# The exponential of an attention step split by head, and its scores issued after its value product

## What is computed

```python
L_q = exterior(q1, q2); L_k = exterior(k1, k2)      # 6 numbers per head and position, of length 1
scores = einsum('bqhc,bkhc->bhqk', L_q, L_k @ _J6.T) * 6.0 ** -0.5
attn = softmax(where(causal, scores, -inf))
out = einsum('bhqk,bkhd->bqhd', attn, v) @ W_out.T  # d = 64
x = x + out + ffn(xn)
```

## Time and profile before

| | |
|---|---|
| time before, median of 2 runs (4733.71 to 4743.04) | 4738.38 us |
| the profiled execution: its time, and the span of its slowest core | 4758.37 us, 4757.3 us |
| spans of the eight cores | 4691.6 to 4757.3 us |
| busy, share of the span: PE, PEld, DVE, ACT, POOL | 60%, 21%, 29%, 31%, 3% |
| exponentials (L580) | 1280, 1120.0 us busy, ScalarE idle before them 2099.5 us |
| value matmuls (L597) | 2560, 1037.8 us busy, TensorE idle before them 842.6 us |
| score matmuls (L557) | 2560, 618.3 us busy, TensorE idle before them 429.4 us |
| masks (L588) | 512, 143.2 us busy |
| divides, first activation (L621) | 128, 130.2 us busy |

### The profile page before, as it was taken

One profiled execution on the slowest core, in us unless ns is written; L12 is line 12 of the kernel. 1 busy time (PEld: TensorE's weight loads), 2 busy tenths in 40 slices (PEclk: granted clock), 3 DMA queues, 4 the chain that ended last, 5 costly groups with the idle time before them and its releaser, 6 DMA issues.

```text
span 4757.3 us, 36021 instructions; the slowest of 8 cores (4691.6 to 4757.3 us)
## 1 busy us (share of the span) xinstructions
PE 2870.3 (60%) x10528; PEld 995.3 (21%) x10528; DVE 1385.6 (29%) x2833; ACT 1475.0 (31%) x1729; POOL 139.4 (3%) x210
## 2 busy tenths in 40 slices
PE   2258555566656855556655865656665586666665
PEld 1115111122112511112211421111221151111112
DVE  4524434322222333332322333332222231111111
ACT  0000144443331034443433014443342203455450
POOL 1200000000000000000000010000000000000001
PEclk9957655567655865566766875556775695555558
DMA  5501310111100320111100041001110021000004
GB/s 110 47 0 54 96 33 27 34 58 62 49 9 7 47 44 27 34 38 62 67 27 11 5 73 34 27 27 56 62 58 7 5 45 36 14 12 14 12 12 73
DMA packets 87144, 180.26 MB, mean 38 GB/s; under 512 B 41760, under 2 KB 42920, under 8 KB 86960
## 3 DMA queue, kind: packets, MB, share of 16 engines
q0 software_dynamic: 56672, 75.38, 8.3%
q1 hardware_dynamic: 30288, 102.58, 7.4%
HBM read 114.36 MB, written 69.73 MB: 39 GB/s over the span
## 4 chain that ended last, share of the span: by engine, by line
PE 44%; DMA 21%; DVE 14%; ACT 12%; issue 7%; DVEq 0%; SPq 0%; ACTq 0%; POOLq 0%; POOL 0%
PE O L597 17%; DMA cdiv<-rscr 10%; DMA y<-ost 7%; PE S L557 7%; PE F L401 5%; ACT exps L580 5%; PE F L437 4%; DMA rscr<-cdiv 3%; DVE oT L639 3%; ACT cdiv L623 3%; ACT cdiv L621 3%; PE F L444 3%; PE F L327 2%; DVE exps L588 1%; DVE stat L278 1%
## 5 line engine op out<-in xcount | busy, mean ns | idle before, releaser
L580 ACT ACTIVATE exps<-S 128x1024 bf16<-128x1024 f32 (+3 forms) x1280 | 1120.0, 894 | 2099.5 <-PE O L597 1354.4
L597 PE MATMUL O<-exps,vaug 128*65 128x512 bf16 (+3 forms) x2560 | 1037.8, 506 | 842.6 <-DVE oT L639 500.1
L557 PE MATMUL S<-fqp,fkp 6*128 6x512 bf16 (+3 forms) x2560 | 618.3, 492 | 429.4 <-ACT exps L580 422.7
L597 PEld LDWEIGHTS O<-exps,vaug 128*65 128x65 bf16 x2560 | 230.3, 136 | 1284.2 <-issue 1265.7
L639 DVE TENSOR_TENSOR oT<-O,cdiv 64x512 bf16<-64x512 f32 x256 | 175.0, 684 | 922.4 <-DMA cdiv<-rscr 916.6
L557 PEld LDWEIGHTS S<-fqp,fkp 6*128 6x128 bf16 x2560 | 141.0, 97 | 1145.4 <-issue 1139.7
L588 DVE TENSOR_TENSOR exps<-exps,tri 128x256 bf16<-128x256 bf16 x512 | 143.2, 290 | 734.9 <-ACT exps L580 732.0
L506 PE MATMUL S<-wout,oT 128*128 128x512 bf16 x1024 | 260.6, 416 | 87.0 <-DVE ost L515 77.6
L401 PE MATMUL F<-wv,xnT 128*128 128x256 bf16 x2048 | 259.0, 291 | 0.6 <-DVE vaug L413 0.3
L307 PE MATMUL F<-idt,xnst 128*128 128x128 f32 x512 | 121.7, 417 | 156.8 <-DVE xnst L294 156.8
L401 PEld LDWEIGHTS F<-wv,xnT 128*128 128x128 bf16 x2048 | 202.0, 103 | 62.6 <-issue 20.9
(11 more groups left out here) (72 smaller groups left out, 1962.6 us busy)
## 6 DMA issues: line engine op xcount, KB each, us to landing
y<-ost POOLq DMA_DIRECT2D x128, 512.0 KB, 5.2
xst<-x SPq DMA_DIRECT2D x64, 512.0 KB, 4.3
x2st<-x SPq DMA_DIRECT2D x64, 512.0 KB, 4.1
cdiv<-rscr SPq DMA_DIRECT2D x128, 256.0 KB, 3.7
wv<-wvT POOLq DMA_DIRECT2D x8, 256.0 KB, 19.8
wout<-woutT POOLq DMA_DIRECT2D x8, 256.0 KB, 20.2
tascr<-qk POOLq DMA_DIRECT2D x16, 128.0 KB, 2.0
rscr<-cdiv SPq DMA_DIRECT2D x128, 4.0 KB
```

The costliest lines, as they stand in the source:

```text
L557: tS.inc(TE.matmul(S_ps[:, ss * 1024 + j * 512 + soff: ss * 1024 + j * 512 + 512], fk_pad[32 * m4:32 * m4 + 6, kt * 128:kt * 128 + 128], f ...
L580: sS.inc(SE.activation(e_out, e_in, AF.Exp))
L597: ins = TE.matmul(O4[:, j * 512 + off:(j + 1) * 512], vaug[:, kt * 1040 + h * 65: kt * 1040 + h * 65 + 65], exp_sb[:, ss * 1024 + j * 512 ...
```

## The change

The body of the step loop in `C_pair` is written anew. The exponential, the mask and the value product are done for one head after the other: two exponentials of up to 512 columns in place of one of up to 1024, two masks of 128 columns in place of one of 256, and a wait of each value matmul for its own head's exponential or mask. Each value matmul counts on its semaphore, where only the second did. S(kt + 2) is issued behind the value product of kt, where it was ahead of it. The buffers, `emit_scores`, the divide and `pace()` are as before. `pace()` is still called at the end of the step.

```diff
             for kt in range(nkt):
                 off = max(kt * 128 - w * 512, 0)
                 ss = kt % 2
-                tS.wait(SE, max(av_snap[kt - 2], sc_snap[kt]))
-                ... (e_out, e_in: both heads, an access pattern of [2, 512 - off])
-                sS.inc(SE.activation(e_out, e_in, AF.Exp))
+                for j in range(2):
+                    base = ss * 1024 + j * 512 + off
+                    end = ss * 1024 + (j + 1) * 512
+                    tS.wait(SE, max(avj.get((kt - 2, j), av_snap.get(kt - 2, 0)), sc_snap[kt]))
+                    sS.inc(SE.activation(exp_sb[:, base:end], S_ps[:, base:end], AF.Exp))
+                    ej = sS.n
+                    if kt >= 4 * w:
+                        sS.wait(VE, ej)
+                        in0 = exp_sb[:, base: base + 128]
+                        mk = vS.inc(VE.tensor_tensor(in0, in0, tri_sb[:, 0:128], OP.mult))
+                        vS.wait(TE, mk)
+                    else:
+                        sS.wait(TE, ej)
+                    if kt == 0 and j == 0:
+                        vS.wait(TE, stx["o4_free"])
+                    m4 = 2 * pr + j
+                    h = 4 * g + m4
+                    tS.inc(TE.matmul(
+                        O4[:, j * 512 + off:(j + 1) * 512],
+                        vaug[:, kt * 1040 + h * 65: kt * 1040 + h * 65 + 65],
+                        exp_sb[:, base:end],
+                        start=(kt == 0), stop=(kt == last_kt)))
+                    avj[(kt, j)] = tS.n
                 exp_snap[kt] = sS.n
+                av_snap[kt] = tS.n
                 if kt + 2 < nkt:
                     emit_scores(kt + 2)
-                if kt >= 4 * w:
-                    ... (one mask of both heads; TensorE waits for it)
-                elif kt + 2 >= nkt:
-                    sS.wait(TE, exp_snap[kt])
-                if kt == 0:
-                    vS.wait(TE, stx["o4_free"])
-                for j in range(2):
-                    ... (the same two value matmuls; tS.inc behind the second)
```

More of the change, by code:

```diff
@@ L569, in C_pair @@
                 stx["pending_div"] = None
+            avj = {}
             for kt in range(nkt):
@@ L602, in C_pair @@
-                tS.inc(ins)
-                av_snap[kt] = tS.n
                 if pace is not None:
```

## The result

| | before | changed |
|---|---|---|
| time, median (runs) | 4742.63 us (10) | 4807.01 us (11) |
| ratio to before, 95% interval | | 1.0147 [1.0124, 1.0170] |
| profiled execution, span of the slowest core | 4757.3 us | 4828.1 us |
| spans of the eight cores, mean | 4723 us | 4804 us |

The change costs 64 us by the medians (70 by the ratio), where 39 were forecast. It stays within 2%, and its interval lies wholly above 1.

The account below looks back on a forecast made before the run. TensorE was taken as the bound at the slow clock, the score-exponential round trip at the fast one. Tail loss of 49 us less 10 gained in fast steps gave +39: 4777 us against the 4738 median, range 4715 to 4835.

Parts of the forecast that it names:

- Full steps, halves, waits: Unmasked steps at the slow clock: stay 1.53 us; half exponentials 0.60 us; extra waits taken as 0, at most 38 us.
- The rule weighed there: ScalarE's exponentials: each split adds some 93 ns, by that alone 119 us over 1280 splits, a sum near 4857.
- The tail: Last masked steps of a pair: late scores add 0.44 us to longer pairs, 0.20 to 4-step pairs, 49 us in all.
- Fast steps: Full steps at the fast clock: halves close the round trip sooner, 1.03 us for 1.10, 144 steps, 10 us gained.
- Moving S(k+2) behind AV(k): Score matmuls issued after value matmuls: middle of a pair unchanged, bill only at its end, +0.44 or +0.20 us per pair.
- The split's worth: Exponential by head: no gain in full slow-clock steps, 10 us gained at the fast clock.
- Round trips vanish: Rival, score matmuls' wait for the exponential: 338 of 422.7 us cost nothing; losing the other 85 gives 4653; chance 0.08.
- A gap between the two heads: Rival, between a step's two value matmuls: the new wait costs 0.14 us, 1280 times, 179 us, giving 4956; chance 0.06.
- ACT becomes the bound: Rival, ScalarE's half exponentials: 4816 if halves don't overlap, 4879 if ScalarE were the bound everywhere; chance 0.04.
- The clock rises: Rival, slow full steps in the last batch and elsewhere: denser TensorE work keeps 2.4 GHz, 192 us gained, 4585; chance 0.02.

Follow-up runs that it names:

- e4: Changed kernel with pace() called between the value product of kt and the scores of kt + 2, so a block follows value matmuls; 1.0030 of the kernel before.
- e2: Kernel before with only the scores of kt + 2 moved behind the value product of kt, exponential and mask left whole; 1.0243 of the kernel before.
- a couple: Split by head in the old order, with two key tiles' scores issued together, then their four value matmuls; four exponential slots, bf16 bias; 0.9443 of the kernel before.

## Why the prediction was right and wrong

**Full steps, halves, waits.** Right. Full steps at 0.50 stay 1.53 us, halves take 0.59, AV of both heads 1.06 as before, so the wait between the heads costs nothing that shows, and the last batch's clock stays 0.50. The rule weighed there, of the Trainium skill, ScalarE: Activation LUTs, section "What ACT_TABLE_LOAD costs", would have put 93 ns on each split, an estimate from its figures. ScalarE's busy time grew by 61 ns each, and none of it lies on the path, as the prediction read from its trace.

**The tail.** Right: 5.69 us for 5.68, 3.70 for "some 3.7", the last batch's stage 709.6 for 708. In the other batches it costs less than taken (28.8 us in e4 for 36), and why is open.

**Fast steps.** Right in size (2.05 us for two, 2.06 forecast). In e4 the full steps of batches 0 to 2 gain 9.6 us, forecast 10, and that is luck in part: a fast step gained 0.04 us where 0.07 was taken, and 6 more steps were fast. In the changed kernel they gain 3.2, because 19 fewer of them per core are fast.

**What failed** is the step *Moving S(k+2) behind AV(k)*. It followed S and AV of the pair, and asked of the clock only whether denser work might raise it. It didn't ask what is queued behind the moved instruction: `pace()` stands at the end of the step, so a block of full-row work that had followed AV now follows S, and its clock rises later. This term was put at nothing. It is +35.6 us in the steps with a block, +44 us in the profiles against e4 (3474.5 - 3430.3) and 55 by the ratios. Less than half of what the steps lost against e4 lies inside the blocks (16.8 of 37.9 us), the rest is S itself, now run at the slow clock. Without the term, e4 stands where the forecast's own terms lead: the tail 14.4 + 28.8, less 9.6 for fast steps, less 7 between pairs and in steps with blocks, +26 in the profiles (14 by the ratio, which goes by the slowest core) where 39 was forecast. The missing term makes it 71 in the profiles. That the measured time still lies inside the stated range is luck: its upper part was made of 38 us for the waits and 20 for the half exponentials and masks, and neither came.

**The split's worth** was under-sized too. As a part by itself it gives 2.2%, where the prediction had 10 us for it at the fast clock and nothing elsewhere: in the old order it shortens the diagonal as well (518.2 us against 557.9), and in the stages with blocks more steps are fast (182.2 against 162.8). The move takes both away.

**The rivals.** "Round trips vanish" was judged rightly: S's wait of 422.7 us is gone, AV's wait for `oT` is 266 us longer, and the two groups' idle time together is 1284 us for 1272. "A gap between the two heads" and "ACT becomes the bound" did not come: 1.06 and an idle 0.44. "The clock rises" looked at the clock, which did move the time, but with the wrong sign and in the wrong stage. The Trainium skill, TensorE: Matmul & The Clock Gate, section "What's actually happening", lets the clock depend on how busy the engine has been of late. The traces agree that it rises in blocks; but the profile's busy share of TensorE is 1.00 in the windows of both kernels, so that share doesn't tell when.

## What to carry to other kernels

When an instruction is moved on an engine's queue, look at what comes to stand behind it, also work that another routine puts there; each new neighbour is a part of the change. A stage's clock belongs in the sum wherever its profile shows both levels, not only where it could be gained. And work that lies in another wait's shadow is free: before moving it out, count what it costs in the open (here 0.67 us, 128 times), and ask whether the wait that makes the shadow can go (here 12% of the time).

## What the hardware showed that was not expected

- With two 6-row matmuls, 0.54 us, between AV and a block, the clock rises 0.46 us later after the block's start for FFN and 1.58 for B1 (2.97 to 3.43, 2.55 to 4.13; in e2 0.60 and 0.36), though TensorE is busy for the whole of the windows shown.
- A change from AV to S and back costs 0.25 us at the slow clock, 0.14 and 0.11 over the columns; a couple saves 3.06 - 2.82 = 0.24 us, about one such change and return.
- With S(2) in the shadow, 4% of the last batch's full steps (6.5 of 168 per core) are fast, where none is before and in the changed kernel. What makes the clock rise in just those pairs is open.
